# The band's mask under the attention maxima: added by VectorE in the instruction that takes the maximum, in place of identity matmuls

## The reference

```
x = ln(x) + pos_emb                                  # 4 x 512 x 128
for l in range(6):
    keys = concat([past, x])                         # one zero token in front: 513 keys
    q, k, v = x @ Wq.T + bq, keys @ Wk.T + bk, keys @ Wv.T + bv
    scores = einsum('bqhd,bkhd->bhqk', q, k) / sqrt(8)
    scores = where((delta >= 0) & (delta <= 125), scores, neg)      # the band
    o = einsum('bhqk,bkhd->bqhd', softmax(scores), v)
    x = ln(x + o @ Wo.T + bo)
    x = ln(x + gelu(x @ W1.T + b1) @ W2.T + b2)
```

## Time and profile before

| | us |
|---|---|
| median of three runs | 1345.5 |
| the profiled execution, its own time | 1351.89 |
| its span, first to last instruction | 1350.1 |
| TensorE busy, in 20080 matmuls | 1058.2 |
| VectorE busy, in 2451 instructions | 804.8 |
| ScalarE busy, in 1419 instructions | 779.0 |
| GpSimd busy, in 544 instructions | 404.6 |
| mean granted TensorE clock | 0.921 |
| first and last maxima reduction (L1008) of the banded units start at | 45.2 and 933.0 |

### The profile page before, as it was taken

One profiled execution on the slowest core, in us unless ns is written; L12 is line 12 of the kernel. 1 busy time (PEld: TensorE's weight loads), 2 busy tenths in 40 slices (PEclk: granted clock), 3 DMA queues, 4 the chain that ended last, 5 costly groups with the idle time before them and its releaser, 6 DMA issues.

```text
span 1350.1 us, 46954 instructions
## 1 busy us (share of the span) xinstructions
PE 1058.2 (78%) x20080; PEld 730.1 (54%) x20080; DVE 804.8 (60%) x2451; ACT 779.0 (58%) x1419; POOL 404.6 (30%) x544
## 2 busy tenths in 40 slices
PE   1466989889898888987989889878656778887835
PEld 0244666666666666665666666656434434544524
DVE  2456667666666677765766666675477765543111
ACT  5144656666666665655666666666445657566532
POOL 4313233332223333322333232333445242202020
PEclk9777999999999999998999999988768879989968
DMA  4211212213211211231221321110201023010110
GB/s 130 47 50 50 50 50 50 51 50 85 47 41 39 79 39 46 50 85 50 50 51 50 85 47 41 41 34 3 48 2 48 7 45 96 10 49 10 48 55 8
DMA packets 72626, 64.79 MB, mean 48 GB/s; under 512 B 16226, under 2 KB 66914, under 8 KB 72418
## 3 DMA queue, kind: packets, MB, share of 16 engines
q1 hardware_dynamic: 72418, 61.78, 17.9%
HBM read 15.70 MB, written 1.05 MB: 12 GB/s over the span
## 4 chain that ended last, share of the span: by engine, by line
PE 44%; ACT 15%; DVE 14%; POOL 8%; issue 8%; SPq 7%; DMA 4%; POOLq 0%; ACTq 0%; DVEq 0%
PE s L530 5%; DVE mx L1008 4%; PE d L647 4%; PE a L511 4%; ACT probs L802 4%; SPq L1492 4%; PE d L730 3%; PE a L430 3%; DMA qpack<-mrows 3%; PE a L637 2%; PE a L719 2%; PE d L545 2%; PE d L430 2%; PE d L557 2%; SPq L1499 2%
## 5 line engine op out<-in xcount | busy, mean ns | idle before, releaser
L802 ACT ACTIVATE probs<-a 128x443 f32<-128x443 f32 (+2 forms) x736 | 358.3, 538 | 273.6 <-PE a L511 270.5
L1008 DVE TENSOR_REDUCE mx<-d 128x2 f32<-128x378 f32 (+1 forms) x768 | 346.8, 510 | 101.3 <-PE d L464 101.2
L530 PE MATMUL s<-probs,vals 128*32 128x189 f32 (+5 forms) x3968 | 191.4, 318 | 14.7 <-ACT probs L802 14.5
L530 PEld LDWEIGHTS s<-probs,vals 128*32 128x32 f32 x3968 | 122.2, 111 | 56.0 <-ACT probs L802 20.1
L511 PE MATMUL a<-qpack,kpack 64*64 64x189 bf16 (+4 forms) x3968 | 143.1, 243 | 0.0
L430 PE MATMUL d<-band,identb 64*64 64x252 bf16 x1152 | 89.5, 301 | 54.1 <-DVE mx L1008 44.4
L464 PE MATMUL d<-kpack,qpack 62*64 62x189 bf16 (+1 forms) x3072 | 128.3, 243 | 0.0
L430 PE MATMUL a<-band,identb 64*64 64x252 bf16 x1152 | 85.0, 285 | 47.3 <-DMA qpack<-mrows 32.0
L1005 DVE TENSOR_REDUCE mx<-d 128x1 f32<-128x512 f32 (+7 forms) x256 | 98.4, 447 | 30.5 <-PE d L479 30.3
L1334 POOL TENSOR_SCALAR veps<-mv 128x4 f32<-128x4 f32 x48 | 11.0, 228 | 327.4 <-DVE mv L1109 327.3
L637 PE MATMUL a<-xmid,w 128*128 128x512 f32 x192 | 94.5, 617 | 4.6 <-ACT hid L880 4.6
(11 more groups left out here) (180 smaller groups left out, 1940.4 us busy)
## 6 DMA issues: line engine op xcount, KB each, us to landing
kpack<-kparts SPq DMA_DIRECT2D x168, 128.2 KB, 3.0
qpack<-qparts SPq DMA_DIRECT2D x168, 128.0 KB, 3.1
qpack<-mrows SPq DMA_DIRECT2D x224, 4.0 KB
w<-in_w SPq DMA_DIRECT2D x12, 256.0 KB, 3.9
w<-in_wa SPq DMA_DIRECT2D x12, 256.0 KB, 3.3
w<-in_wb SPq DMA_DIRECT2D x12, 256.0 KB, 3.5
rowt<-in_rowt SPq DMA_DIRECT2D x6, 384.0 KB, 3.4
stream<-in_x SPq DMA_DIRECT2D x4, 256.0 KB, 4.0
```

The source lines that it names most:

```text
L530: mm = pe.matmul(s_ps[32 * j:32 * j + 32, q0:q0 + w - skip], vals[:, u % 2, at:at + 32], probs[:, n % SETS, j, col + skip:col + w], start= ...
L802: act.activation(probs[:, n % SETS, j, 0:width], a_ps[A.bank("exp", u, v, b)][:, 0:width], ACT.Exp, scale=SCALE).then_inc(a_emptied, 1)
L1008: red = dve.tensor_reduce(out[:, 2 * tb:2 * tb + 2], bank[:, 0:2 * width].rearrange("p (t k) -> p t k", k=width), AX.X, ALU.max)
```

## The change

VectorE reads the fp32 table `bands` beside the bank, adds it and takes the maximum, tile by tile, with `tensor_tensor_reduce`; the sum is written back over the bank. TensorE's mask matmuls in `maxima` are gone (four of 64x252 or 64x258 columns for every two banks, 1536 in all), and its first query x key matmul into each tile overwrites what the bank held. One reduction over two tiles becomes two `tensor_tensor_reduce` calls over one tile each.

```
+LOWEST = -3.0e38
...
             def maxima(u, couple, tp):
                 buf, banks = wait_maxima(u, couple, tp)
-                for e, h in quarters():
-                    rows = slice(64 * e, 64 * e + 64)
-                    if tp:
-                        edges(banks[e], e, h)
-                    else:
-                        pe.matmul(banks[e][64 * h:64 * h + 64, 0:2 * (P + 1)], identb[rows, rows],
-                                  band_first[rows, :, :].rearrange("p t k -> p (t k)"),
-                                  start=True, stop=False, skip_group_check=True)
                 width = SPAN if tp else P + 1
...
-                                       start=False, stop=True, skip_group_check=True)
+                                       start=True, stop=True, skip_group_check=True)
...
                 else:
                     width = SPAN if tb else P + 1
-                    red = dve.tensor_reduce(out[:, 2 * tb:2 * tb + 2],
-                                            bank[:, 0:2 * width].rearrange("p (t k) -> p t k", k=width), AX.X, ALU.max)
+                    for n in range(2):
+                        first = 0 if tb else SPAN + n * (P + 1)
+                        red = dve.tensor_tensor_reduce(bank[:, n * width:(n + 1) * width], bank[:, n * width:(n + 1) * width],
+                                                       bands[:, first:first + width], 1.0, LOWEST, ALU.add, ALU.max,
+                                                       accum_out=out[:, 2 * tb + n:2 * tb + n + 1])
                 red.then_inc(d_emptied, 1)
```

## The result

The changed kernel takes **1391.5 us** (median of four runs, 1387.9 to 1397.3) beside 1345.8 us for the kernel before on the same chip: a ratio of 1.034, 95% interval 1.030 to 1.038. It is slower by 46 us. The forecast was slower, 1418 us, with a range of 1355 to 1500: the sign and the mechanism hold, the size was 1.6 times too large (73 us against 46). The profiled execution took 1397.3 us, span 1395.5. One execution of an experiment further down was in a slower state of the chip; times and ratios leave it out.

What follows compares the result with a forecast made beforehand. VectorE was taken to bound part A of each unit, a TensorE and ScalarE chain part B. 22.4 units x 3.8 us = 85, less 12 hidden, gave +73 us: 1425 profiled, 1418 us as median, range 1355 to 1500.

Steps and rivals of the forecast that it cites:

- What bounds the kernel: A 34.8 us unit: part A, 20.1 us, is VectorE's already; part B, 14.7 us, is TensorE's and ScalarE's chain.
- D: VectorE's growth per bank against the kernel before, from start to start; forecast 0.27 us.
- The price of a pair: On VectorE, one tile's add with maximum plus accumulator read: 0.275 + 0.09 = 0.365 us for 189 columns.
- low bound: A pair at 0.305 us, D = 0.15; the chain's 15 banks give 2.25 - 1.5 = 0.7 us a unit, 1360 us.
- the forecast's formula: Growth per unit: part A's 22 banks times D, less 1.65 us of rest and 0.53 of masks: +3.8 us.
- The 1.65 us of rest that it eats: VectorE's rest in part A, the unit's 20.1 us stretch, taken to absorb that much of the 5.94 us growth.
- In part B two lie on the chain: 0.53: In part B, 14.7 us of TensorE and ScalarE chain, removing two mask steps saves 0.53 us a unit.
- What hides the growth: TensorE's 32.0 us of waits for the DMA returning the maxima cover some growth; 12 us taken off.
- Nothing overlapping behind the add: Rival 1, on VectorE: the accumulator read waits for the full add, a pair 0.434 us, D = 0.41; 1487 us, chance 0.20.
- The cheap pair: Rival 2, on VectorE: D is 0.05, masks off the chain win, 1327 us; turns at a 0.28 us pair; chance 0.07.
- Half rate: Rival 3, on VectorE: the accumulating form takes two cycles a column, a pair 0.56 us; about 1600 us, chance 0.05.
- rival 4: The granted clock, taken as 0.8 for the banded part: 1468 us, chance 0.08.

Runs made afterwards that it cites:

- change in ten steps: The change made only in steps 0, 3, 4, 5, 6, 11 to 15 of a unit's sixteen, the rest as in the kernel before: 1394.9 us, ratio 1.0350.
- the other six: The change made only in steps 1, 2, 7, 8, 9, 10 of a unit's sixteen, the rest as in the kernel before: 1340.7 us, again 1341.2.
- two reductions: Kernel before with each bank's reduction cut into two tensor_reduce of one tile each, no mask on VectorE: 1356.8 us, ratio 1.0065.
- no mask: Kernel before without the mask matmuls under the banded units' maxima, VectorE's reductions unchanged: 1343.0 us, ratio 0.9954.
- add only: Changed kernel with a plain tensor_tensor add in place, the maximum left out and `mx` set to zero once: 1354.3 us, ratio 1.0039.
- sum to SBUF: Changed kernel with the sum written to an SBUF tile instead of over the bank, in the first 20 of 24 units: 1364.8 us, ratio 1.0092.
- both: Changed kernel with all mask matmuls put back, so the mask is added twice: 1386.7 us, ratio 1.0282; again 1389.1 us, 1.0304.
- ten masks: Changed kernel with the mask matmuls kept too in ten of sixteen steps (0, 3, 4, 5, 6, 11 to 15): 1386.6 us, ratio 1.0279.

## Why the prediction was right, and where its sizes were off

**What bounds the kernel.** Right, and shown three ways: with the change in ten steps the whole loss is there, with it in the other six there is a gain, and 0.38 of the dose (D 0.063 against 0.165), without any mask on VectorE, gives about as much of the unit's growth (1.0 us against 2.4 to 2.6).

**The price of a pair.** This is the step that failed most. "I take 0.09" for the accumulator read, and 0.275 for the add, made 0.365; measured 0.3125. The add alone is 0.261, 0.014 less than worked out from the rows of 512 and 256 columns. ScalarE's read was a poor model: there what follows starts 0.09 us after the read (1122.61 to 1122.70 us), on VectorE the next add starts with the read (both at 542.28 us). Part of the difference was given back by a cost that no row of before hinted at: "I take no difference" for the write into PSUM was wrong in this form (0.0375 us a pair), though right for a plain add. D became 0.165 instead of 0.27. The forecast's own low bound, D = 0.15, was much nearer than its middle; but the time that it was given there, 1360 us, used the 1.5 us of masks and was wrong by 30.

**From the price to the unit.** With D = 0.165 the forecast's formula gives 22 x 0.165 - 1.65 - 0.53 = 1.45 us a unit; measured 2.4. Over 22.4 units, less 12 us, that is 20 us and a time of 1366, 25 too low. So the forecast came as near as it did because a price that was too high met terms that were too kind; that part is luck. Two terms were too kind. "The 1.65 us of rest that it eats": 0.67 of it stayed, since VectorE still has to wait there for a value copy and a maxima step. "In part B two lie on the chain: 0.53": the unit with and without masks differs by 0.2, and part B is as long as before (37.2 - 22.6 = 14.6 us against 14.65), since at one more step TensorE waits for VectorE. With two reductions the formula fails outright: 22 x 0.063 = 1.4 us would vanish in 1.65 of rest, and the unit grew by 1.0. What fits all runs to about 0.3 us, most of them to 0.1, is the number of banks on the chain, 15, with 0.4 us for masks that are gone:

| run | D, us | masks on TensorE | 15 D - masks, us | unit less 34.8, us |
|---|---|---|---|---|
| no mask | 0 | gone | -0.4 | -0.4 |
| add only | 0.062 | gone | 0.5 | 0.6 |
| two reductions | 0.063 | kept | 0.9 | 1.0 |
| sum to SBUF | 0.09 | gone | 1.0 | 1.1 |
| both | 0.165 | kept | 2.5 | 2.6 |
| change in ten steps | 0.165 | part | 2.1 to 2.5 | 2.6 |
| the change | 0.165 | gone | 2.1 | 2.4 |

The 0.4 is taken from the first row; the others test it.

**What hides the growth.** 12 us were taken; the DMA wait fell by 16.5, and over twenty units the stalls beyond the shortest unit by 10. Right in kind and size.

**The rivals.** Nothing overlapping behind the add: false, 0.3125 against 0.434. The cheap pair: its turning point, 0.28 us, was just passed with the sum in SBUF (0.275), and that run is 0.9% slower than before, so the point itself was wrong, for the same reason: masks on the chain don't come back. Half rate: false; the accumulating form takes 387 ns for 189 columns and 326 for 129, which is 1.0 ns a column, as in the rows without accumulation (1.04). One of its sources is in PSUM; the form with both in SBUF was not run. The clock (rival 4, 1468 us, chance 0.08): real, but small. No run shows the 0.8 that this figure takes for the banded part: in the changed kernel the granted clock from 143.9 to 906.2 us is 0.97. Single falls of some 3 us cost 1.2 us each where they meet part B. That the accumulating operation is two instructions the trace shows, with 1536 reads of 139 ns beside 1536 adds; in series a pair takes only 0.05 us more than the plain add (0.3125 against 0.261).

**What was to be seen.** 1536 adds of about 355 and 293 ns: 387 and 326. VectorE's share of the chain over 30%: 33%. TensorE's wait over 100 us: 106.0. A unit of 38 to 39 us: 37.2. The time behind unchanged: about; 5.7 us of the span's growth lie after the twenty units.

## What to carry to other kernels

Work moved from the busier engine to one with a third of its time free still lands on the path (46 us here) if it stands where that engine is the one waited for: read one period of the timeline, find the stretch in which the receiving engine never rests, and count what you add there. A piece on the chain can be worth far less than its length (36 us promised, 6 found); a cheap run that takes it out with nothing in its place tells what it is worth before a replacement is paid for. And where the price and the place can be chosen per step, put the new form only into the receiver's rest, and count the new price from start to start, never by the length of the row.

## What the runs showed of the hardware that was not expected

- VectorE's accumulator read (139 ns in its row) starts together with the next add (both at 542.28 us). With the sum in SBUF a pair takes 0.275 us, only 0.014 more than a plain add in place in PSUM (0.261).
- An accumulating add that writes to PSUM, followed by the read's write to SBUF, costs 0.0375 us a pair more than with both in SBUF (0.3125 against 0.275 us; rows of the add of 387 against 350 ns). A plain add in place in PSUM (0.261 us) doesn't show it.
- With fewer matmuls some of those that are left ran slower: two projections took 2.08 us instead of 1.12. Without masks in the two steps ahead of the projections, 12 of 60 units (the change twice, ten masks) were 1.2 us longer with a fall of the clock there, to 0.57 over the 4 us shown. With masks in these two steps (all masks twice, the change in ten steps) none of 60 was, and the same place showed 1.00 with masks that nobody needs. Units of any length with a granted clock below 0.8 in their last 3 us are 19 of 60 against 5 of 60.
